# The output gate of a post-norm decoder layer: twelve of 28 tiles of x2 turned by a transposing load

## The reference

```
x = _layernorm(x + attention(x))
x = _layernorm(x + cross_attention(x, ctx))            # this is x2
def step(c, xt):
    ft = sigmoid(xt @ wf.T + c @ uf.T + bf)
    it = sigmoid(xt @ wi.T + c @ ui.T + bi)
    gt = tanh(xt @ wc.T + c @ uc.T + bc)
    return ft * c + it * gt
c_final = scan(step, c0, x)                            # over the 16 sequences
h = tanh(x @ wo.T + c_final @ uo.T + bo)
return _layernorm(x + h)
```

## Time and profile before

| | |
|---|---|
| time, median of 3 runs | 1435.63 us (1434.34 to 1437.33) |
| the profiled execution's own time | 1437.93 us |
| its span, first to last instruction | 1435.8 us |
| mean granted TensorE clock | 0.993 |
| busy: PE, DVE, ACT, POOL | 98%, 64%, 50%, 37% |
| DMA, all stages | 157.71 MB, mean 110 GB/s |
| output gate, first add to last add | 1350.31 to 1426.43 us |

### The profile page before, as it was taken

The page is one execution under the profiler, slowest core; times in us unless marked ns, Lnnn a source line. Parts: engine busy times, 40 slices in busy tenths (PEclk is TensorE's granted clock), DMA queues, the critical chain, the costliest instruction groups (busy, mean ns, idle before and its releaser), DMA issues.

```text
span 1435.8 us, 28331 instructions
## 1 busy us (share of the span) xinstructions
PE 1404.1 (98%) x10022; PEld 1214.8 (85%) x10022; DVE 919.3 (64%) x1912; ACT 716.9 (50%) x1959; POOL 525.3 (37%) x423
## 2 busy tenths in 40 slices
PE   6999999999999999999999999999999999999997
PEld 3677777777789999999999988999999999999775
DVE  4578888888765677667757763544554445546687
ACT  4477777777546655665566554322222222222232
POOL 2454555455366565656565622000000000010265
PEclk9999999999999999999999999999999999999999
DMA  6123222234466666666666946010110101000353
GB/s 191 37 67 92 78 89 89 77 89 130 138 161 192 193 198 214 213 196 193 214 210 201 218 132 179 1 26 1 26 26 0 26 0 32 30 0 31 96 183 125
DMA packets 133050, 157.71 MB, mean 110 GB/s; under 512 B 62386, under 2 KB 70578, under 8 KB 132980
## 3 DMA queue, kind: packets, MB, share of 16 engines
q1 hardware_dynamic: 132980, 156.78, 37.0%
HBM read 105.38 MB, written 35.78 MB: 98 GB/s over the span
## 4 chain that ended last, share of the span: by engine, by line
PE 90%; issue 4%; POOL 3%; DVE 2%; SPq 0%; ACT 0%; DMA 0%; POOLq 0%; DVEq 0%
PE banks L1464 15%; PE banks L1493 10%; PE banks L971 9%; PE banks L955 9%; PE banks L316 7%; PE banks L984 6%; PE banks L941 6%; PE banks L1495 5%; PE banks L284 5%; PE banks L265 3%; PE banks L296 2%; PE banks L271 2%; PE banks L244 2%; PE banks L927 2%; POOL o_r L2039 1%
## 5 line engine op out<-in xcount | busy, mean ns | idle before, releaser
L442 ACT ACTIVATE s_p<-banks,a_nmax 112x224 f32<-112x224 f32 (+1 forms) x512 | 198.8, 417 | 94.3 <-DVE a_nmax L536 94.3
L714 POOL TENSOR_TENSOR s_p<-s_p,a_rinv 112x896 f32<-112x896 f32 (+1 forms) x128 | 165.0, 1310 | 166.6 <-DVE a_rinv L544 161.0
L1438 POOL CAST m_hi<-w_raw 128x2048 fp32r<-128x2048 f32 x1 | 2.3, 2267 | 407.7 <-PE banks L1464 407.7
L1581 ACT ACTIVATE f_gate<-f_gate 128x448 f32<-128x448 f32 x90 | 52.2, 580 | 198.6 <-DVE f_gate L1704 198.6
L1701 DVE TENSOR_TENSOR f_gate<-banks,f_xg_early 128x448 f32<-128x448 f32 x45 | 28.1, 625 | 189.6 <-PE banks L1495 189.6
L1309 POOL TENSOR_TENSOR x_cx_lo<-s_cx_raw,x_cx_hi 125x512 fp32r<-125x512 f32 x96 | 120.9, 1294 | 38.0 <-ACT x_cx_hi L1081 38.0
L551 DVE COPY a_pt<-banks 112x448 f32<-112x448 f32 x128 | 79.4, 620 | 61.4 <-PE banks L284 61.2
L442 ACT ACTIVATION_READ_ACCUMULATOR s_p<-banks,a_nmax 112x1 f32 x512 | 113.9, 222 | 0.0
L284 PEld LDWEIGHTS banks<-identity,s_p 112*112 112x112 f32 x768 | 86.4, 135 | 30.5 <-POOL s_p L714 9.3
L284 PE MATMUL banks<-identity,s_p 112*112 112x112 f32 x768 | 106.2, 262 | 0.9 <-DVE a_pt L551 0.9
L535 DVE TENSOR_REDUCE a_nmax<-banks 112x1 f32<-112x224 f32 x256 | 97.2, 380 | 12.6 <-PE banks L271 12.3
(11 more groups left out here) (251 smaller groups left out, 3641.6 us busy)
## 6 DMA issues: line engine op xcount, KB each, us to landing
s_ct_raw<-in_ct SPq DMA_DIRECT2D x16, 1500.0 KB, 6.7
s_cx_raw<-in_cx SPq DMA_DIRECT2D x16, 1500.0 KB
a_xt<-in_xt SPq DMA_DIRECT2D x16, 448.0 KB, 3.8
a_xrow<-in_x SPq DMA_DIRECT2D x16, 448.0 KB, 3.7
a_xres<-in_x SPq DMA_DIRECT2D x16, 448.0 KB, 4.7
x_scratch<-a_xn SPq DMA_DIRECT2D x16, 448.0 KB, 3.2
x_scratch<-x_xn SPq DMA_DIRECT2D x16, 448.0 KB, 4.6
x_halves<-x_halves SPq DMA_DIRECT2D x16, 448.0 KB, 3.4
```

Of the source, the lines that this page charges most:

```text
L442: e = act.activation((p1 if c else p0)[:, g, h, :], src, ACT.Exp, bias=nmax[:, g % 2, c, h:h + 1], accum_out=rsum[:, g % 2, c, h:h + 1])
L714: pool.tensor_tensor(p[:, g, :, :], p[:, g, :, :], inv, ALU.mult).then_inc(norm_done, 1)
```

## The change

From tile 5 on every second tile (5, 7, ... 27, twelve in all) isn't turned by PE. It is loaded a second time, from `x2_halves`, by a transposing load into one of three SBUF buffers (`landing`), and the high and low halves are made from there. The row load of these tiles stays, since the residual needs it. SP issues the first three transposing loads (tiles 5, 7, 9) behind the 14 pieces of the base, and each later one ahead of the row load of the tile three before it; it waits until the low half of the tile six before it is made (and all before that one). Four semaphores are merged into two: `base_mm` into `base_done`, and `stats_done`, `mv_done`, `veps_done` into `moments_done`.

```diff
+    FIRST_LOADED, LANDING = 5, 3
...
+        landing = sb("landing", [P, LANDING, KC, P])
+        def by_load(n):
+            return n >= FIRST_LOADED and n % 2 == 1
+        def landing_slot(n):
+            return (n - FIRST_LOADED) // 2 % LANDING
+        def turned_by_pe(n):
+            return sum(not by_load(i) for i in range(n + 1))
+        def x2_turned(n):
+            return landing[:, landing_slot(n), :, :] if by_load(n) else turn_bank(n)
...
-        base_mm = sem("base_mm")
+        landed = [sem(f"landed{i}") for i in range(LANDING)]
...
+            def load_turned(n):
+                if n >= TILES or not by_load(n):
+                    return
+                if n >= FIRST_LOADED + 2 * LANDING:
+                    sp.wait_ge(xtl_done, n - 2 * LANDING + 1)
+                sp.dma_start_transpose(landing[:, landing_slot(n), :, :].bitcast(U16), x2_half_rows[2 * P * n:2 * P * n + 2 * P, :])\
+                  .then_inc(landed[landing_slot(n)], 16)
...
-            sp.wait_ge(base_done, 1)
+            sp.wait_ge(base_done, 2)
             for j in range(TURNS):
                 for p, q, t, n in pieces(j):
                     sp.dma_start(turned[p:p + n, j, :], base[t:t + n, q, :]).then_inc(turned_in[j // 2], 16)
+            for n in range(FIRST_LOADED, FIRST_LOADED + 2 * LANDING):
+                load_turned(n)
             for n in range(SLOTS, TILES):
+                load_turned(n + 3)
                 load(n)
                 store(n - SLOTS)
...
         def turn(pe, n):
-            if n >= TILES:
+            if n >= TILES or by_load(n):
                 return
...
         def xth(act, n):
-            act.wait_ge(xt_done, n + 1)
+            if by_load(n):
+                act.wait_ge(landed[landing_slot(n)], 16 * ((n - FIRST_LOADED) // 2 // LANDING + 1))
+            else:
+                act.wait_ge(xt_done, turned_by_pe(n))
             if n >= 2:
                 act.wait_ge(o_done, n - 1)
-            act.activation(xt_hi[:, n % 2, :, :], turn_bank(n), ACT.Copy).then_inc(xth_done, 1)
+            act.activation(xt_hi[:, n % 2, :, :], x2_turned(n), ACT.Copy).then_inc(xth_done, 1)
...
-            dve.tensor_tensor(xt_lo[:, n % 2, :, :], turn_bank(n), xt_hi[:, n % 2, :, :], ALU.subtract).then_inc(xtl_done, 1)
+            dve.tensor_tensor(xt_lo[:, n % 2, :, :], x2_turned(n), xt_hi[:, n % 2, :, :], ALU.subtract).then_inc(xtl_done, 1)
```

More of the change, by code:

```diff
@@ L1793, in recurrence, with output_gate @@
         return Stage(sync, tensor, scalar, vector, gpsimd)
-def output_gate(nc, io, x2, out, identity, cc, banks, wo, uo, closing):
+def output_gate(nc, io, x2, x2_halves, out, identity, cc, banks, wo, uo, closing):
     P = 128
@@ L1847, in output_gate @@
         r_done = sem("r_done")
-        stats_done = sem("stats_done")
-        mv_done = sem("mv_done")
-        veps_done = sem("veps_done")
+        moments_done = sem("moments_done")
         rstd_done = sem("rstd_done")
@@ L1856, in output_gate @@
         out_rows = out.rearrange("b t d -> (b t) d")
+        x2_half_rows = x2_halves.rearrange("b t d -> (b t) d")
         def pieces(j):
@@ L1918, in product @@
             elif n < BANKS:
-                pe.wait_ge(base_done, 1)
+                pe.wait_ge(base_done, 2)
             else:
@@ L1958, in tensor @@
                         i += 1
-            mm.then_inc(base_mm, 1)
+            mm.then_inc(base_done, 1)
             for n in range(3, TILES):
@@ L1992, in statistics @@
                 dve.wait_ge(r_done, n + 1)
[L1993 to L1997, removed]
+                dve.bn_stats(stats[:, s, :], r[:, s, :]).then_inc(moments_done, 1)
+                dve.wait_ge(moments_done, 3 * n + 1)
+                dve.bn_aggr(mv[:, s, :], stats[:, s, :]).then_inc(moments_done, 1)
+                dve.wait_ge(moments_done, 3 * n + 2)
+                dve.tensor_scalar(veps[:, s, :], mv[:, s, 1:2], EPS, None, ALU.add).then_inc(moments_done, 1)
             def norm(n):
@@ L2008, in vector @@
             xtl(dve, 3)
-            dve.wait_ge(base_mm, 1)
+            dve.wait_ge(base_done, 1)
             dve.wait_ge(bo_in, 16)
@@ L2043, in power @@
                     return
-                pool.wait_ge(veps_done, n + 1)
+                pool.wait_ge(moments_done, 3 * n + 3)
                 if n >= 4:
@@ L2247, in decoder @@
         third = recurrence(nc, io, x2_halves, identity, cc, raw, raw_in, opening, closing, banks)
-        fourth = output_gate(nc, io, x2, out, identity, cc, banks, opening.w[0], opening.w[1], closing)
+        fourth = output_gate(nc, io, x2, x2_halves, out, identity, cc, banks, opening.w[0], opening.w[1], closing)
         block = ctx.enter_context(nc.Block())
```

## The result

The changed kernel takes 1448.48 us (median of 4 runs, 1445.78 to 1448.98) against 1434.99 for the kernel before, timed beside it (4 runs): ratio **1.0092, 95% interval 1.0080 to 1.0104**, 13.5 us slower. The forecast was 7.6.

A forecast was written before the change was run, and what follows sets the result against it. PE's 3.22 us a tile was taken to set the last stage's pace from about tile 7. First add 1360.1 + DVE work 65.7 + waits 8.2 = 1434.0, 7.6 later; 1435.63 + 7.6 = 1443.2 us, range 1438.5 to 1451.5.

The forecast's parts named there:

- Start, 9.8 us: Last stage's first add waits for tile 5's load, issued behind the base's pieces: 1360.1 against 1350.31, 9.8 us later.
- The landing of 3.8: Tile 5's transposing load, issued at 1355.06, was taken to land in 3.8 us, with ends of 2.6 and 8.1.
- The half clock into product 5: After some 10 us idle, PE runs product 5 at half speed, 5.3 us; DVE waits 1.6 before subtract 7.
- The subtract and the copy now read SBUF for 12 tiles ... so I count nothing: Loaded tiles' subtract with both inputs in SBUF was priced at 0.686 us against 0.68 now, so no added cost.
- Waits of 8.2: DVE's waits from first to last add: 1.2 + 1.6 + 1.2 + 1.0 + 3.2 = 8.2 us.
- my 73.9: Forecast stretch from first to last add in the last stage: 73.9 us.
- The turns: Last stage's PE transposes, on the path; dropping 12 of 24 saves PE 6.7 us, DVE at most 5.5.
- The other queues at nothing: SP's 12 added issues, DMA traffic and merged semaphores cost nothing; row loads have some five steps of slack.
- No change: Rival: DVE sets the pace, last add 0.4 us later, 1436.0; needs DVE waits under 3.5 us; chance 0.07.
- A gain: Rival: the 5.5 us of DVE's waits for PE won without a start shift, 1430; chance 0.02.
- SP as the bound: Rival: transposing issues take 4.4 us, delaying tile 8's row load and product 7; about 1451; chance 0.10.
- A crossbar at 1.3 a block: Rival: eight blocks in turn make a tile's load 10.5 us, the end slips 57 us to 1493; chance 0.01.

The follow-up runs named there:

- e1: Changed kernel with the loaded tiles beginning at 7 instead of 5, three loads ahead of tile 8's row load; ratio 1.0055 to the kernel before.
- e4: Changed kernel with 42 further matmuls of unused result in PE's gap ahead of product 5; ratio 1.0082 to the kernel before.
- e2: Kernel before, no transposing loads; the subtract of tiles 5, 7, ... 27 reads the SBUF row slot instead of PSUM; ratio 1.0011.
- e3: Changed kernel with all loads and ACT copies; the subtract of loaded tiles reads a stale PSUM bank instead of landing; ratio 1.0056 to the kernel before.
- e5: Changed kernel with all transposing loads issued, but PE turns every tile and nothing reads landing; ratio 1.0055 to the kernel before.
- e9: Changed kernel with even tiles from 8 loaded, ACT copying them to PSUM for DVE's subtract, row loads one step earlier; ratio 0.9999 to the kernel before.
- e8: Changed kernel with even tiles from 8 loaded, POOL making their low halves, the next lead rounded up; ratio 1.0043 to the kernel before.
- e12: e9 with table LEAD staying at 3 to step 13 and 2 to step 25; 1433.9 against 1435.97 us for the kernel before, ratio 0.9981.

## Why the prediction was right in side and wrong in size

- **Start, 9.8 us: right.** 9.83 measured, with the landing (3.8), the order on SP and the first add as worked out. e1 takes the load of tile 5 away and has the first add back at 6.5. The landing of 3.8 was taken from larger transposing loads on the ground that these take longer than plain ones; in the changed kernel the two kinds land in 3.5 and 3.6 in the median, so that ground didn't hold, though the number did.
- **The half clock into product 5: right.** The clock and the wait of 1.6 are there, and e4 gives the 1.6 back.
- **"The subtract and the copy now read SBUF for 12 tiles ... so I count nothing": this step failed.** The copy's 619 against 582 ns make 0.4 us of ACT in twelve tiles, and DVE's waits for ACT are those forecast. The subtract is not 0.69 but about 1.2 in 9 of 12 tiles, and DVE's busy time rose by 4.0. The earlier trace rows showed the right operation in the wrong company: it is the last tile's, when POOL has no residual to make; only a power of one column ran beside it. The shape of an operation and where its operands lie don't give its price; what runs beside it does. e2 shows the cause without a load, e3 shows the time without the cause. By the Trainium skill ("SBUF — State Buffer", Who interferes with whom) a VectorE instruction with two SBUF inputs contends with a GpSimd instruction that reads SBUF. The trace agrees: the subtract's 0.68 became 1.2 and the power's 0.55 became 1.0. I had not weighed that rule, and it was the one that spoke against this change.
- **Waits of 8.2: came out at 10.3.** 4.4 for PE where I had 3.2, 1.4 for POOL where I had 1.2, and 1.6 under no name where I had 1.0. In e3 DVE's idle time is 8.7, so three quarters of the excess go with the long subtracts, and its stretch is 74.25 against my 73.9. In the changed kernel PE idles for 2.10 near 1403 and is then granted the lower clock, an add waits 1.47, and in e3 none of this happens.
- **The turns: right that they are on the path, their share not isolated.** e3 is 1.9 us shorter from add to add than the kernel before despite the half clock; but PE also waits 1.0 less there for a row load (0.4 against 1.4), and what part of the 1.9 that is wasn't measured apart.
- **The other queues at nothing: right by the wrong cover.** I named slack of some five steps, and for the row load of tile 8 a landing well ahead of turn 8. e5 shows 7.9 us once tile 5 isn't late: what covered the row load of tile 8 was the wait at the start.
- **Rivals.** No change would have needed waits of DVE under 3.5 us; they were 10.3. A gain would have needed tile 5 landed ahead of the first add's old place; its load was only issued 4.8 us behind that place. SP as the bound (issues of 4.4) didn't happen; 1.28 was measured. A crossbar at 1.3 a block is excluded with 3.5 for a tile of eight.

Sum: 4.0 (busy) + 2.1 (waits) = 6.1 over the forecast. The forecast had the direction, the start and the place of the loss right; of the stretch behind the start it had the sign wrong, since it put at nothing the one cost that outweighs the turns.

## What to carry to other kernels

Before an operand is moved from PSUM to SBUF, look at what the neighbour (here POOL) reads from SBUF at that moment, and take the price from a row where the two overlap. A load put into one ordered queue delays everything behind it (5.6 us for the row load of tile 8 in e5), and that can be hidden by the very stall that the same load causes. When work leaves the engine that sets the pace, look at the order that feeds it (here the table LEAD): in e9 the gain turned into idle time, and the new table alone won 3.8 us of the stretch.

## What the runs showed of the hardware

- Mostly it is the instruction that starts second that is slowed: DVE's subtract inside POOL's residual took 1.2 us, the residual stayed at 1.29, and POOL's power of one column inside that subtract took 1.0. BATCH_NORM_STATS2, with one SBUF input, stayed at 0.69 beside residuals, but in e8 a normalisation with one tile from SBUF went from 0.54 to 1.39. Two normalisations of e8 don't fit the order: at 1409.74 and 1423.43 they started 0.07 and 0.09 us ahead of a residual by the trace, and took 1.65. By the Trainium skill ("SBUF — State Buffer", Who interferes with whom) tensor_scalar can enter a mode that takes the shared port pair; e8's row agrees.
- PE's clock fell also with short gaps in a busy stretch: 2.10 us of idling (after), 2.30 (e4) and 1.80 (e9) each came with 3.4 us at the lower level. 1.41 in the kernel before and 1.64 in e9 did not. Nor did 3.23 in e8, ahead of 1361.31, where the granted clock was 1.00 from add to add: the length of the gap alone doesn't decide it.
- ACT reads the same tile from SBUF in 0.619 us and from PSUM in 0.582.
- A transposing load of 256 KB took SP 1.28 us to issue and 3.5 to land. Plain row loads of the same size took 0.43 and 2.8 in the kernel before, but 3.6 to land in the changed kernel, beside the new loads, and in e12 both kinds landed in 3.5. So the transposing load is dear to issue, and no slower to land than a plain one in the same kernel.
